# One sum of eight key tiles per group of heads instead of two sums of four: seven tiles added by GpSimd, the eighth by an accumulating transfer

## The reference

```python
q = (x @ Wq + bq).reshape(B, N, NUM_HEADS, HEAD_DIM)     # 16 heads of 32
k = (y @ Wk + bk).reshape(B, M, NUM_HEADS, HEAD_DIM)
v = (y @ Wv + bv).reshape(B, M, NUM_HEADS, HEAD_DIM)
scores = jnp.einsum('bnhd,bmhd->bhnm', q, k) * scale
attn = jax.nn.softmax(scores, axis=-1)
out = jnp.einsum('bhnm,bmhd->bnhd', attn, v).reshape(B, N, IMAGE_DIM)
```

## Time and profile before

| | us |
|---|---|
| median of 3 runs | 3074.13 |
| the profiled execution | 3071.63 |
| its span on the core | 3069.8 |
| PE busy | 2977.9 (97%) |
| VectorE busy | 2220.0 (72%) |
| GpSimd busy | 1962.5 (64%) |
| ScalarE busy | 1679.1 (55%) |

### The profile page before, as it was taken

One profiled execution on the slowest core, in us unless ns is written; L12 is line 12 of the kernel. 1 busy time (PEld: TensorE's weight loads), 2 busy tenths in 40 slices (PEclk: granted clock), 3 DMA queues, 4 the chain that ended last, 5 costly groups with the idle time before them and its releaser, 6 DMA issues.

```text
span 3069.8 us, 40867 instructions
## 1 busy us (share of the span) xinstructions
PE 2977.9 (97%) x15216; PEld 1818.9 (59%) x15216; DVE 2220.0 (72%) x3368; ACT 1679.1 (55%) x2920; POOL 1962.5 (64%) x682
## 2 busy tenths in 40 slices
PE   7999999999999999999999999999999877899999
PEld 4666666666666666666666666666534333344477
DVE  7777777777777777777777777777746899986653
ACT  1566666666666666666666666666641555320021
POOL 1699898989989898988989898989850000000000
PEclk9999999999999999999999999999999989999999
DMA  6423332232223233332223222332240122224100
GB/s 165 122 53 78 71 76 63 63 85 67 73 53 90 61 94 98 76 86 53 73 61 91 56 70 66 85 74 53 47 156 29 43 68 97 67 70 166 69 14 18
DMA packets 99817, 230.10 MB, mean 75 GB/s; under 512 B 22754, under 2 KB 27874, under 8 KB 98114
## 3 DMA queue, kind: packets, MB, share of 16 engines
q1 hardware_dynamic: 99044, 226.71, 27.8%
q10 hardware_dynamic: 576, 0.79, 0.1%
HBM read 114.46 MB, written 8.06 MB: 40 GB/s over the span
## 4 chain that ended last, share of the span: by engine, by line
PE 90%; DVE 6%; ACT 1%; POOL 1%; issue 1%; DMA 0%; SPq 0%; ACTq 0%; DVEq 0%; POOLq 0%
PE ps L1819 17%; PE ps L1858 15%; PE ps L1845 15%; PE ps L1772 9%; PE ps L1796 9%; PE ps L1803 9%; PE ps L2065 4%; PE ps L2029 4%; PE ps L1873 4%; PE ps L2045 3%; DVE bx L1308 1%; PE ps L1827 1%; POOL psum L896 1%; PE ps L2057 1%; ACT V L1516 1%
## 5 line engine op out<-in xcount | busy, mean ns | idle before, releaser
L1046 DVE TENSOR_REDUCE pm<-ps 128x1 f32<-128x512 f32 x2048 | 1407.4, 691 | 571.7 <-PE ps L1819 499.1
L1527 ACT ACTIVATE pf<-ps 128x512 f32<-128x512 f32 x2048 | 1216.6, 599 | 721.8 <-PE ps L1845 626.7
L896 POOL TENSOR_TENSOR psum<-psum,pf 128x2048 f32<-128x2048 f32 x254 | 1167.7, 4597 | 70.3 <-ACT pf L1527 57.7
L1819 PE MATMUL ps<-ks,qs 96*128 96x512 f32 x2048 | 844.0, 412 | 4.9 <-DVE pm L1046 2.3
L1845 PE MATMUL ps<-qs,ks 98*128 98x512 f32 x2048 | 812.8, 398 | 2.8 <-ACT pf L1527 2.6
L896 POOL TENSOR_TENSOR psum<-pf 128x2048 f32<-128x2048 f32 x127 | 581.5, 4579 | 80.2 <-ACT pf L1527 79.0
L1819 PEld LDWEIGHTS ps<-ks,qs 96*128 96x128 f32 x2048 | 386.6, 189 | 262.6 <-issue 198.7
L1858 PE MATMUL ps<-pf,V 128*32 128x512 f32 x4096 | 492.7, 598 | 0.0
L1845 PEld LDWEIGHTS ps<-qs,ks 98*128 98x128 f32 x2048 | 390.6, 191 | 50.0 <-ACT pf L1527 12.4
L908 POOL PARTITION_ALL_REDUCE qstat<-qstat x2 | 0.7, 366 | 608.5 <-DVE qstat L1344 608.5
L1796 PE MATMUL ps<-cTh,Wkg 128*128 128x512 f32 x732 | 292.7, 400 | 2.6
(11 more groups left out here) (223 smaller groups left out, 3004.3 us busy)
## 6 DMA issues: line engine op xcount, KB each, us to landing
ks<-KH SPq DMA_DIRECT2D x512, 128.0 KB, 2.4
ks<-KL SPq DMA_DIRECT2D x256, 128.0 KB, 2.4
cT<-in_ctxT SPq DMA_DIRECT2D x32, 768.0 KB, 4.8
Wkg<-wk_rows SPq DMA_DIRECT2D x61, 384.0 KB, 3.1
BC<-bc_rows SPq DMA_DIRECT2D x32, 512.0 KB, 4.8
ring<-in_ffn_w SPq DMA_DIRECT2D x16, 1024.0 KB, 7.8
wA<-in_W_fcT SPq DMA_DIRECT2D x4, 1024.0 KB, 10.0
wB<-in_W_projT SPq DMA_DIRECT2D x4, 1024.0 KB, 7.0
```

Of the source, the lines that this page charges most:

```text
L896: pool.tensor_tensor(acc, before, pf[:, tile % P_SLOTS, :], ALU.add).then_inc(s_sum, 1)
L1046: dve.tensor_reduce(pm[:, n // BLK, n % BLK:n % BLK + 1], src, AX.X, ALU.max).then_inc(s_wfree, 1)
L1527: act.activation(pf[:, tile % P_SLOTS, j * NTOK:(j + 1) * NTOK], ps[:, S_BANK + u % S_BANKS, :], ACT.Exp, scale=SCALE).then_inc(s_exp, 1)
L1819: last = pe.matmul(dst, qs[0:3 * HD, h, t * P:(t + 1) * P], ks[0:3 * HD, keys_of(of, j), i * 512:(i + 1) * 512], start=True, stop=True)
```

## The change

GpSimd now adds the tiles 0 to 6 of a group (6 adds) into one accumulator, waits for the exponentials of tile 7, and issues a transfer that adds tile 7 (1 MB, SBUF to SBUF, `accum_op=ALU.add`) to the accumulator. `sums` comes once per group, waits for that transfer (`s_tail`), and stands in the burst at step 16 of the next group (before: at steps 24 of the group itself and 8 of the next). `pf` has 5 slots; ACT waits for the transfer before it overwrites tile 7, at tile 4 of the next group. `rescale` comes behind the issue of the transfer; `D` comes 16 steps later, and so does the save of a batch's outputs. The last group has 3 adds, one `sums`, and four tiles of `last_sums` as before.

```diff
-D_LAG = 1
+D_LAG = 17
-LOW_AT = {2: (0, 0), 3: (1, 2)}
-P_SLOTS = 4
+LOW_GROUP = 1
+LOW_AT = {0: 0, 5: 1}
+P_SLOTS = 5
-NSUM = 4
-RUNS = NGT * MT // NSUM
-CHUNK_RUNS = NG * MT // NSUM
-ADDS = NSUM - 1
-STEPS = (NGT - 1) * UPG + T_LAG + 2
+ADDS = MT - 2
+KEEP_ADD = 3
+LAST_SUMMED = 4
+LAST_ADDS = LAST_SUMMED - 1
+SUM_BURST = MT // BURST + 1
+STEPS = (NGT - 1) * UPG + T_LAG + D_LAG + 1
...
-            for run in range(RUNS - 1):
-                if low_at(run, 0):
-                    low_context(*low_at(run, 0))
-                if run * NSUM % MT == MT - NSUM:
-                    rescale(run * NSUM // MT)
-                acc = psum[:, run % 2, :]
-                if run >= 2:
-                    pool.wait_ge(s_den, run - 1)
-                for n in range(ADDS):
-                    tile = NSUM * run + n + 1
+            for g in range(NGT):
+                adds = ADDS if g < NGT - 1 else LAST_ADDS
+                acc = psum[:, g % 2, :]
+                if g >= 2:
+                    pool.wait_ge(s_den, g - 1)
+                for n in range(adds):
+                    if low_at(g, n):
+                        low_context(*low_at(g, n))
+                    tile = g * MT + n + 1
...
-                    pool.wait_ge(s_sum, run * ADDS + (n + 1))
-                    if n == 0 and low_at(run, 2):
-                        low_context(*low_at(run, 2))
-                if run % (MT // NSUM) == 0 and run // (MT // NSUM) + 1 < NGT:
-                    keep_max(run // (MT // NSUM) + 1)
+                    pool.wait_ge(s_sum, g * ADDS + (n + 1))
+                    if n == KEEP_ADD - 1 and g + 1 < NGT:
+                        keep_max(g + 1)
+                if g < NGT - 1:
+                    pool.wait_ge(s_exp, HG * (g + 1) * MT)
+                    pool.dma_start(acc, pf[:, (g * MT + MT - 1) % P_SLOTS, :], accum_op=ALU.add
+                                   ).then_inc(s_tail, 16)
+                    rescale(g)
...
-                    old = tile - P_SLOTS
-                    act.wait_ge(s_pv, (old + 1))
-                    act.wait_ge(s_sum, old // NSUM * ADDS + max(old % NSUM, 1))
+                    of, r = divmod(tile - P_SLOTS, MT)
+                    act.wait_ge(s_pv, of * MT + (r + 1))
+                    if r < MT - 1:
+                        act.wait_ge(s_sum, of * ADDS + max(r, 1))
+                    else:
+                        act.wait_ge(s_tail, 16 * (of + 1))
...
-                pe.wait_ge(s_sum, (run + 1) * ADDS)
+                if g < NGT - 1:
+                    pe.wait_ge(s_tail, 16 * (g + 1))
+                else:
+                    pe.wait_ge(s_sum, g * ADDS + LAST_ADDS)
...
-                run, rest = divmod(BURST * n, NSUM)
-                if n > 0 and rest == 0 and run < RUNS:
-                    sums(run - 1)
+                g, rest = divmod(n - SUM_BURST, MT // BURST)
+                if g >= 0 and rest == 0:
+                    sums(g)
```

More of the change, by code:

```diff
@@ L166, in high_at, with low_at @@
     return [(c, half, f) for f in range(KC)] if half is not None and c < NB * NCH else []
[L169 to L173, removed]
+def low_at(g, n):
+    c = g // NG + 1
+    if g % NG == LOW_GROUP and n in LOW_AT and c < NB * NCH:
+        return c, LOW_AT[n]
+    return None
 LEAD_SIDE, LEAD_WORK, LEAD_IN = lead_in()
@@ L356, in emit @@
         s_sum = sem("s_sum")
+        s_tail = sem("s_tail")
         s_den = sem("s_den")
@@ L713, in _ @@
                     stack_keys(g + SIDE_AHEAD)
-                if g == NGB:
-                    save_out(0)
                 if g == 0:
@@ L727, in _ @@
                     max_rows(g + 1)
+                if g == NGB:
+                    save_out(0)
                 if g == NGT - 2:
@@ L1535, in take_sums @@
             def take_sums(c):
-                act.wait_ge(s_den, CHUNK_RUNS * (c + 1))
+                act.wait_ge(s_den, NG * (c + 1) + (c == NB * NCH - 1))
                 act.copy(dt_[:], ps[:, DEN_BANK, :]).then_inc(s_dt, 1)
@@ L1572, in _ @@
                     take_out(i // UPG - 1)
-                if i % (NG * UPG) == BURST * HG + 1 and i // (NG * UPG) > 0:
+                if i % (NG * UPG) == BURST * HG * (SUM_BURST - MT // BURST + 1) + 1 and i // (NG * UPG) > 0:
                     take_sums(i // (NG * UPG) - 1)
@@ L1861, in values, with sums @@
                 last.then_inc(s_pv, 1)
[L1863 to L1867, removed]
+            def sums(g):
+                first = g % NG == 0
+                if g == 0:
                     pe.wait_ge(s_sel, NG + 1)
-                if first and run > 0:
-                    pe.wait_ge(s_dt, run // CHUNK_RUNS)
-                pe.wait_ge(s_sum, (run + 1) * ADDS)
+                if first and g > 0:
+                    pe.wait_ge(s_dt, g // NG)
+                if g < NGT - 1:
+                    pe.wait_ge(s_tail, 16 * (g + 1))
+                else:
+                    pe.wait_ge(s_sum, g * ADDS + LAST_ADDS)
                 for j in range(HG):
                     last = pe.matmul(ps[j * HD:(j + 1) * HD, DEN_BANK, :], sel[:, g % NG, :],
-                                     psum[:, run % 2, j * NTOK:(j + 1) * NTOK], start=first,
-                                     stop=(run % CHUNK_RUNS == CHUNK_RUNS - 1))
+                                     psum[:, g % 2, j * NTOK:(j + 1) * NTOK], start=first,
+                                     stop=(g % NG == NG - 1 and g < NGT - 1))
                 last.then_inc(s_den, 1)
             def last_sums():
-                for tile in range(NGT * MT - NSUM, NGT * MT):
+                for tile in range(NGT * MT - MT + LAST_SUMMED, NGT * MT):
                     for j in range(HG):
@@ L1891, in burst @@
                         values(tile)
-                run, rest = divmod(BURST * n, NSUM)
-                if n > 0 and rest == 0 and run < RUNS:
-                    sums(run - 1)
+                g, rest = divmod(n - SUM_BURST, MT // BURST)
+                if g >= 0 and rest == 0:
+                    sums(g)
                 if n == BURSTS - 1:
+                    sums(NGT - 1)
                     last_sums()
```

## The result

| | median us | runs | ratio to the kernel before, 95% interval |
|---|---|---|---|
| before | 3075.14 | 3073.68 to 3076.24 (4) | |
| changed | 3054.20 | 3053.43 to 3057.0 (4) | 0.9934 [0.9917, 0.9951] |

What follows compares the result with a forecast made beforehand. PE was taken to bound the attention without a gap: 63 products gone, -54.2, plus 13 of low-context waits gives -41; 3071.6 becomes 3030.6, median 3033 us. Forecast's own range 3020 to 3045, for all cases 3015 to 3130.

Steps and rivals of the forecast that it cites:

- tight group: Second group of each chunk, holding the low context's second half; transfer issued one add later, leaving 9.5 us instead of 12.2.
- the wait for the low context: PE's K pieces in each chunk's second group wait 0.9 us for POOL's low context, in 15 chunks: 13 us.
- The issue: POOL issuing the accumulating transfer, 63 times; each was taken to hold POOL for 1.0 us.
- At 9.3 it lands 0.2 us inside the tight window of 9.5: Transfer in each chunk's second group: 8.3 us plus 1.0 for issuing, landing in time, no stall beyond the 0.9 us.
- tight window: Each chunk's second group, from issue at 989.9 to the landing limit at 999.4: 9.5 us without further loss.
- the contention: Added to the transfer's time for key stacking beside it, with DMA engines at 0.50: 1.5 us.
- both reads counting: Accumulating transfer moves tile and accumulator one after the other: 1.8 + 5.0 = 6.8 us; counted once, 4.3.
- The rule of the rival: Late transfer: with L from issue to landing, loss 15 x (L - 9.5) + 48 x (L - 12.2); slower from L = 12.2; chance 0.23.
- a sign of being wrong: DMA packets of half the size and twice the count that hold up the key stacking; no size given.
- eaten in part: Transfer landing 9.5 to 12.2 us after issue eats part of the gain; 3055 us at 11; chance 0.21.
- What moves at no cost: Rescaling, D, batch 0's save, the fifth slot and the attention's end change place or order; net cost taken as 0.
- behind the last maxima: Attention's end, paced by POOL's adds: +1 and -1 within 3 us, taken as 0.

Runs made afterwards that it cites:

- e11: Changed kernel with e1's and e2's edits and PE multiplying the eighth tile in each chunk's second group and the last group but one; 3023.7 us.
- e10: Changed kernel with half the columns of the sixth add left out in each chunk's second group, so the transfer is issued earlier there; 3038.7 us.
- e5: Changed kernel without the third of the three copies that stack each group's keys, from the fourth group on; 3043.8 us.
- e3: Changed kernel with the accumulating transfer taken out and the eighth tile left out of the sums; 3027.7 us.
- e1: Changed kernel with VectorE negating the maxima by a reduction instead of a product with -1; 3054.4 us.
- e2: Changed kernel with the second half of the low context one add earlier, behind the fourth add of the chunk's second group; 3047.7 us.
- e7: Changed kernel with the transfer taken back in each chunk's second group, where PE multiplies the eighth tile itself; 3040.3 us.

## Why the prediction was right in direction and half right in size

**Right.** PE bounds the attention, and a product that goes is worth 0.86 us where nothing else is late: the third period lost 0.86, and e11, with 46 products gone, is 46.8 us under its own median of before (3070.5; 46 x 0.86 = 39.6, and the shorter tight period makes 15 x 0.35 = 5.3 of the rest). In a normal group POOL has room. The tight group was the right place to look, and the wait for the low context was sized well: 0.9 us in 15 places forecast, 0.68 in 15 measured (10.2 us, forecast 13). The issue, 0.9 us of POOL's time in all, was nearly the 1.0 taken. In the normal groups no transfer is waited for, as forecast, except for the last one of the attention (5.1 us of ACT).

**The step that failed first: "At 9.3 it lands 0.2 us inside the tight window of 9.5 [...] no stall on top of the 0.9".** It lands after 10.4 us and ACT goes on after 10.5, and e10, which issues it 2.3 us earlier there, won 15.5 us. The mis-sized term is the contention, 1.5 us. Without it the forecast was 1.8 + 5.0 + 1.0 = 7.8, and the groups that are not tight measured 7.9; with it, 9.3 were forecast and 10.4 measured, so the contention is 2.5. The row that it was read from misleads. The mean of 0.50 in the earlier trace rows is made of a stretch in which the DMA engines do nearly nothing and one in which they are at 0.80, and the tight window lies in the busy kind. The kernel before, with its DMA share and GB/s in the last two columns:

```profile
1020.00:1026.00 6.00, 6.00 (x34) 4.12 (x36) 5.45 (x9) 5.15 (x10) 4.25 (x2) 1.00 0.09 12
1026.00:1034.00 8.00, 8.00 (x54) 5.80 (x46) 5.50 (x9) 4.18 (x7) 6.80 (x3) 1.00 0.80 190
989.90:999.40 9.50, 9.50 (x64) 6.34 (x63) 6.76 (x10) 5.71 (x11) 9.34 (x3) 1.00 0.74 174
```

The third row is the forecast's tight window itself. The stacking does not begin "in the middle" of it, as the prediction says, but 2.3 us in, and the load of the K weights 0.6 us in.

The slope speaks for both reads counting: from the half to the whole transfer it takes 3.4 us more in the median (4.6 to 8.0), where 2.5 per further 0.5 MB moved was assumed for double reads and 1.25 for a single one. The Trainium skill's rule in "Collectives: The Full Stack", on the bandwidth ceiling, that a reducing transfer is half as fast as a copy, was on the right side, and the trace is slower still. Two sizes alone don't show that a second read is the cause.

**The path was wrong too, and the rule's fit is luck.** The rule of the rival, 15 x (L - 9.5), makes 15 us with 10.5, which looks like e10's 15.5. But the window was reckoned 0.9 us too short: it takes off both sums that are gone and forgets the new one, which stands in the burst just ahead of the K unit (995.23 and 996.82 in the timeline above). With 10.4 the rule gives 1.5 us, and that is what the trace has on its path: PE idles 1.8 us for the copy of V and 0.4 for the transfer. The other 9.1 us are waits for the stacked keys. The prediction looked only at what the stacking does to the transfer, and the transfer does as much to the stacking, 7.5 us became 11.7. This was listed as a sign of being wrong, without a price; e5 shows that it is worth 0.64 of the 1.04 us per tight period. The rival "eaten in part" named 3055 at L = 11, near the measured 3054.2, but by the path that cost little.

**A term that was missing: the first period, 0.91 us x 15 = 13.6.** "What moves at no cost" counted POOL's instructions and not what stands on the other engines while they run. The issue, which was to fit into POOL's spare room, moves POOL's add over the moment in which DVE negates the maxima, and DVE is blocked until the add ends (0.73 us in the median instead of 0.17). Without the issue, in e3, this happens in one group of 64; with the reduction of e1 the fourth and first period together fall from 67.95 to 67.11, which is 12.6 of the 13.6 us.

**The sum again:** 54.2 - 10.2 (low context) - 15.5 (late transfer and keys) - 13.6 (DVE's product) = 14.9, and 3.2 behind the last maxima, where I had taken 0: 18.1, as the spans differ. The terms can be added like this only because they were all measured in one kernel. Taken away singly they are worth 6.5 (e2), 15.5 (e10) and 0 (e1), and e1 with e2 is again 0. That the late keys and DVE's product both hang on the transfer is shown by e3: without it PE's waits for both are gone from the two periods but one of 1.9 us.

## What to carry to other kernels

Work that is taken from the bound engine and given to the next one is worth its full price only as long as that one has room in every group, not in the mean: POOL's 31 us per group plus the low context made 34.2 against 33.5. Its share in the mean hides that, and so did the mean DMA share of a window that was half empty. Where the relief misses in one group of four, keep it in three and leave the fourth as it was (e7: 16 products more, 14 us less). And as long as a second engine sets the pace at one place, test every other edit with this place mended: e1 and e2 won nothing together before it and 13 us after.

## What the runs showed of the hardware

- An accumulating transfer within SBUF, issued by GpSimd, 1 MB: 7.0 us at least, 8.0 in the median of all, 10.4 in the median where a load of 384 KB and the stacking of keys begin 0.5 and 2.1 us after its issue, 7.9 where they begin 2.7 and 4.3 us after it (e10); 0.5 MB: 4.6. The row of its issue lasts 0.88 us at either size, the next operation starts 0.6 us after it, and the two operations behind take 0.3 us longer each (1.08 to 1.38, 4.58 to 4.89): 0.9 us in all.
- It slows small copies that run beside it: the 12 issues of a group's keys (128 KB each) that took 7.5 us took 11.7, at a DMA share of 1.01, and the last copy landed 13.8 us after the first issue instead of 9.4.
- A VectorE product of 128x16 numbers that began beside a GpSimd add of 4.6 us ended with the add, after up to 2.4 us instead of 0.17; the same by a reduction took 0.17 always.
